# Making the fourth feed-forward sequence's products during the last steps of the latent attention

## The reference

```python
x = x + _L0_xattn_ref(_layernorm(x), ctx_512, ctx_512)
x = x + _L0_ffn_ref(_layernorm(x), ...)                  # routed experts
x = x + _L1_xattn_ref(_layernorm(x), ctx_512, ...)       # latent attention, 16 heads
x = x + _L1_ffn_ref(_layernorm(x), w_gate, w_up, w_down) # this case is about its start
```

```python
gate = _mx_linear(x, w_gate)        # 256 -> 1024
up = _mx_linear(x, w_up)
inter = jax.nn.silu(gate) * up
return _mx_linear(inter, w_down)    # quantises inter, 1024 -> 256
```

## Time and profile before

| | |
|---|---|
| median of 3 runs | 785.99 us |
| lowest and highest | 784.54, 786.02 us |
| the profiled execution, its own time | 785.92 us |
| its span, from the first to the last instruction | 783.9 us |
| busy, share of the span: PE, DVE, POOL, ACT | 94%, 75%, 72%, 52% |
| mean granted clock of TensorE | 0.991 of full speed |

### The profile page before, as it was taken

The page is one execution under the profiler, slowest core; times in us unless marked ns, Lnnn a source line. Parts: engine busy times, 40 slices in busy tenths (PEclk is TensorE's granted clock), DMA queues, the critical chain, the costliest instruction groups (busy, mean ns, idle before and its releaser), DMA issues.

```text
span 783.9 us, 15005 instructions
## 1 busy us (share of the span) xinstructions
PE 733.1 (94%) x4872; PEld 534.6 (68%) x4872; DVE 589.0 (75%) x1077; ACT 405.2 (52%) x1084; POOL 564.7 (72%) x588
## 2 busy tenths in 40 slices
PE   3999999978999999798999999999999999987896
PEld 2655555446888888766787777777777777755554
DVE  5898888948777778776565677676767676768996
ACT  1678878732333233326454454655455544573664
POOL 5667777525777767665757778888788888766895
PEclk9999999979999999999999999999999999999999
DMA  9300000013000001132110000000000000000101
GB/s 252 136 1 0 0 0 1 2 52 127 21 21 21 20 22 59 37 125 102 51 52 1 1 2 1 2 1 1 1 1 2 2 1 2 1 1 2 35 28 48
DMA packets 8764, 24.14 MB, mean 31 GB/s; under 512 B 1711, under 2 KB 5167, under 8 KB 8087
## 3 DMA queue, kind: packets, MB, share of 16 engines
q1 hardware_dynamic: 8154, 23.28, 9.0%
q10 hardware_dynamic: 549, 0.08, 0.1%
HBM read 21.26 MB, written 2.10 MB: 30 GB/s over the span
## 4 chain that ended last, share of the span: by engine, by line
PE 44%; DVE 6%; issue 3%; ACT 3%; POOL 2%; DVEq 0%; POOLq 0%; ACTq 0%
PE ps L1413 17%; PE ps L1462 5%; PE ps L1483 4%; PE ps L1429 4%; PE ps L1447 4%; PE ps L1432 3%; PE ps L1497 3%; PE ps L1324 2%; DVE ps L2172 1%; DVE f_h L2160 1%; ACT p L1573 1%; POOL f_h L2280 1%; ACT f_gated L2124 1%; PE ps L2046 1%; ACT l_y L1563 0%
## 5 line engine op out<-in xcount | busy, mean ns | idle before, releaser
L1758 POOL TENSOR_TENSOR q<-turned 64x512 f32<-64x512 f32 x127 | 166.2, 1309 | 24.2 <-DVE turned L1677 11.4
L1413 PE MATMUL ps<-l_yt,a 128*128 128x512 f32 x576 | 144.1, 400 | 4.0 <-DVE a L1631 2.3
L1413 PEld LDWEIGHTS ps<-l_yt,a 128*128 128x128 f32 x576 | 105.1, 189 | 28.9 <-DVE a L1631 2.9
L1745 POOL TENSOR_TENSOR p<-p,l_inverse 128x512 f32<-128x512 f32 x64 | 66.4, 1040 | 60.1 <-DVE l_inverse L1699 59.2
L1677 DVE TENSOR_TENSOR turned<-ps,rope 128x1024 f32<-128x1024 f32 x64 | 78.0, 1219 | 40.6 <-PE ps L1413 36.3
L881 PE MATMUL ps<-yt_experts,wsplit 128*128 (+1 forms) x384 | 97.3, 403 | 0.1
L468 DVE TENSOR_REDUCE negmax<-ps 128x4 f32<-128x512 f32 x128 | 85.1, 685 | 14.9 <-PE ps L291 13.8
L1573 ACT ACTIVATE p<-ps,l_negmax 128x128 f32<-128x128 f32 x256 | 89.8, 388 | 6.5 <-DVE l_negmax L1668 6.5
L881 PEld LDWEIGHTS ps<-yt_experts,wsplit 128*128 128x128 f32 x384 | 71.6, 193 | 14.5 <-DVE inner L1036 0.3
L384 ACT ACTIVATE pt<-ps 128x512 f32<-128x512 f32 x128 | 69.8, 599 | 5.5 <-PE ps L313 3.7
L1590 ACT ACTIVATE qs<-ps 128x512 f32<-128x512 f32 x32 | 19.1, 597 | 102.6 <-PE ps L1432 102.6
(11 more groups left out here) (231 smaller groups left out, 1563.0 us busy)
## 6 DMA issues: line engine op xcount, KB each, us to landing
wide<-in_wide SPq DMA_DIRECT2D x8, 768.0 KB, 4.3
mx_raw<-in_mx SPq DMA_DIRECT2D x8, 384.0 KB, 3.1
x<-in_x SPq DMA_DIRECT2D x4, 512.0 KB, 8.9
ctx_t<-in_ctx_t SPq DMA_DIRECT2D x1, 2048.0 KB, 7.8
out<-x SPq DMA_DIRECT2D x16, 128.0 KB, 1.7
narrow<-in_narrow SPq DMA_DIRECT2D x8, 192.0 KB, 4.1
ktraw<-in_ctx_rows SPq DMA_DIRECT2D x1, 1248.0 KB
wraw<-in_gate SPq DMA_DIRECT2D x1, 1024.0 KB, 18.7
```

Of the source, the lines that this page charges most:

```text
L1413: out = pe.matmul(tile_bank(n, k), a[i][:, pa, kin, k * 128:(k + 1) * 128], yt[j % 2][:, py, kin, :, :].rearrange("p b s -> p (b s)"), sta ...
L1745: pool.tensor_tensor(p[:, head, :, :], p[:, head, :, :], spread(inverse[:, head, :], 2, S), ALU.mult).then_inc(normed[head], 1)
L1758: t = pool.tensor_tensor(out[rows[(head + half) % 2], head, :], turned[rows[head], half, :], turned[rows[head], 2 + half, :], ALU.add)
```

## The change

`EARLY` goes from 3 to 4. On PE the gate products of sequence 3 come ahead of `turn_p(END)`, its up products ahead of `project(END)`; they go to the banks 0 and 7, so they no longer wait for the last context's split, which `products(4, 1)` does now. The first turning, of `hq(0)`, waits for `combine(3)` instead of `combine(2)`. `combine(3)` reads its two up banks in two halves. On ACT `silu(3)` and `invert_scale(2)` are written ahead of the loop, where they stood as the loop's first instructions: the order of ACT's queue is the same.

```diff
@@ feed_forward
-    EARLY = 3
+    EARLY = 4
     gate_bank = lambda n, half: m.bank(2 + half)
     up_bank = lambda n, half: m.bank((0, 7 if n < EARLY else 1)[half])
@@ tensor
         products(2, 0)
         products(2, 1)
+        products(3, 0)
         turn_p(END, 0)
         turn_p(END, 1)
         project(END - 1, 0)
         project(END - 1, 1)
         context(END)
+        products(3, 1)
         project(END, 0)
         project(END, 1)
         steps(pe, body)
@@ scalar, body
             if n >= EARLY and inside(n, B):
                 silu(n)
-            if n >= 3 and inside(n - 1, B):
+            if n >= EARLY and inside(n - 1, B):
                 invert_scale(n - 1, (place - 1) % 4)
@@ scalar
         keep_context(END)
+        silu(3)
+        invert_scale(2, 2)
         steps(act, body)
```

## The result

The changed kernel takes 782.45 us in the median of 5 runs (781.26 to 783.34) where the kernel before takes 785.99 (784.54 to 787.58): ratio 0.9947, 95% interval 0.9928 to 0.9966, so 0.5% faster, 3.5 us. The forecast was 786.2, no difference that can be told, and its range ended at 783.2. It came out as rival 1, and somewhat better than that rival's 783.3.

A forecast was written before the change was run, and what follows sets the result against it. DVE and POOL were taken to set the pace in the feed-forward's steady run. SiLU(3)'s 3.2 us gain is swallowed by waiting for POOL; net +0.2 to +0.3 on 785.92 gives 786.2, range 783.2 to 786.9.

The forecast's parts named there:

- rival 1: `clip(1)` on DVE gets between POOL's `hq(0)` and sequence 2's quantising; `combine(3)` 1.61 earlier, -2.7 us, 783.3; chance 0.27.
- L2221's fate: At `clip(1)`: DVE waits for both overlapping POOL instructions, as the late rescaling had; it ends at 715.20, `combine(3)` +0.25.
- The other bound: At `clip(1)`: DVE gets between the two POOL instructions, ending at 712.26 + 1.08 = 713.34.
- pause of 3.25 us: PE idles 713.2 to 716.45 before the turning of `hq(0)`; clock falls there, back for `down(0)`; net +0.2 us.
- The head: Steps up to `combine(3)`: `turn_p(END)` at 706.58, +1.12; SiLU(3) at 710.65, 3.2 us earlier.
- the winning branch: The case of rival 1, `clip(1)` getting between the POOL instructions: `combine(3)` at 713.26, -1.61 us.
- The two pauses in PE: If `clip(1)` gets between the POOL instructions, PE pauses 0.8 and 1.4 us, so the clock stays up and `down(0)` is fast.
- The clock: If PE's clock stays up for `down(0)`, DVE and POOL give back later idle time, up to 1.1 us.
- Rival 3: After a 3.25 us pause PE stays at 1.2 GHz twice as long, over sequences 5 and 6: +3.1, 789.1; chance 0.05.

The follow-up runs named there:

- experiment 2: The changed kernel with the lower limit of `clip(1)` taken from PSUM instead of SBUF, run twice: 780.30 us (ratio 0.9920), then 781.69 (0.9936).

## Why the prediction was wrong, point by point

| drain, us | kernel |
|---|---|
| 81.6 | before; `combine(3)` at +14.8 from `combine(0)`; clock falls ahead of `down(0)` |
| 80.1 | before with both pauses filled; `combine(3)` at +14.8; clock stays up |
| 78.6 | after; `combine(3)` at +13.2; clock stays up |
| 77.9 | after, `clip(1)` with one SBUF input; `combine(3)` at +12.5 |

- **The step that failed** is "I choose L2221's fate: `clip(1)` waits for both, 714.12 + 1.08 = 715.20". It got between: 711.99 + 1.08 = 713.07. The other bound had it at 713.34, 0.3 later as all times of that profile are. One lost contest was taken for a property of two POOL instructions that overlap in the record. The rescaling, the instruction that had lost, won the same contest in the changed kernel, with POOL's first half running for 0.56 us instead of 0.24. The Trainium skill's rule of issue order (SBUF — State Buffer, section "Who interferes with whom") gave the right outcome at `clip(1)`; L2221 contradicts it only if the start on record of a POOL instruction is also the moment of its issue, which no run here shows.
- **What followed from it** fell too: no pause of 3.25 us, so no fall of the clock at 716.
- **The head** was right on the winning branch: `combine(3)` 1.61 earlier was forecast for rival 1, and 1.58 measured against `combine(0)` (13.24 against 14.82). SiLU(3) and `turn_p(END)` stood at 710.32 and 706.28, with the 0.3 offset 710.6 and 706.6 for a forecast of 710.65 and 706.58. The quantising of sequence 1 took 1.92, as the forecast chose, and not the 2.13 of before. The two pauses in PE were given as 0.8 and 1.4 and measured 1.44 and 1.45.
- **The clock** was seen, with the right sign, and sized too small: at most 1.1 us, the idle time of DVE before `combine` and before the clip. Measured with the order unchanged: 81.57 to 80.11, 1.46. Of that 0.6 are gained by `combine(6)` and 0.2 more by `combine(15)`, within the 1.1. The last 0.65 come at the end, where the rescaling wins against POOL (1.58 instead of 2.90) and DVE comes 0.56 instead of 0.24 us after POOL's first half. That term was missing: the wait was inside a DVE instruction's duration and not in any idle time. In the changed kernel the three parts are 1.58 (`combine(3)`), 0.75 (from there to `combine(15)`) and 0.66 (from there to the end), 2.99 in all; rival 1 had 1.55 and 1.1 and nothing for the last, so it came near the time partly by luck.
- **Half and half**: of the 3.0 us of drain 1.5 come from the clock and 1.5 from the earlier `combine(3)`, if the pauses are filled first and `combine(3)` is moved then. The other order was seen only in part, in the gate products alone: with the clock down an earlier `combine(3)` gave nothing. In medians: 2.0 (786.25 to 784.25) and 1.8 (784.25 to 782.44). Each of these two steps is clear of the noise. The medians say more than one pair of profiles on the first half, because the clock falls in different places from execution to execution.
- **Rival 3** (twice as long at 1.2 GHz) did not come in the changed kernel, but did in the one with the gate products alone, where the old pause of 2.8 us was left: the granted clock was down between 718 and 726 us instead of between 719 and 724. It cost 1.1 us from `combine(3)` to the end (67.85 instead of 66.75), not the 3.1 that the rival gave it.
- **The two halves of the change do different things.** The gate products bring the SiLU forward, the up products let `combine(3)` follow and shorten the pause ahead of `down(0)`. In medians each gains alone, 1.1 and 2.0 us, against 3.5 and 3.8 for both; the intervals are too wide to say that together they give more than their sum.

## What to carry to other kernels

An instruction that reads two SBUF tensors on VectorE beside a busy GpSimd can hold a wait that shows only in its duration (here 1.94 instead of 1.21 us, and 2.90 instead of 1.22): compare its duration with others of its form, and give it a PSUM operand if one is at hand. Who wins such a contest is no constant of the pair; from one row both outcomes stay open, and the chance should say so. And where TensorE is not the bound, its pauses can still count: here what kept its clock up was worth as much as what shortened the path.

The best version that came out is the changed kernel with the limit of `clip(1)` in PSUM: 780.3 and 781.7 us in two jobs, ratios 0.9920 and 0.9936.

## What the runs showed of the hardware that was not expected

- 21 unused matmuls in TensorE's pauses made the kernel 2.0 us faster (786.25 to 784.25). From 700 us on, the pause of 2.83 or 2.84 us was followed by a granted clock of 0.50 in all five profiles that have it unfilled, the one of 2.25 in three of five, the one of 2.53 not in its one profile, and pauses of 0.5 to 1.5 in none (falls behind the last copy to x left aside). The length of a single pause does not decide it alone: in the profile of before the granted clock is 0.50 from 167 to 177 us, and the pauses just ahead were 1.10 (ending at 164.08) and 1.41 (ending at 166.79).
- The place of the fall varies with the execution: the profiles of the kernel before and its near relatives have it at 711, at 718 or at 720 us. The kernel's times spread with the mean granted clock, which counts falls elsewhere too: of 73 runs of the kernel before, 39 had 0.991 and a median of 787.1 us, 30 had 0.993 and 785.6, 2 had 0.996 and 783.1, and 2 had 0.989 and 786.7.
- Two profiles of the changed kernel agree to some 0.03 us from 700 us on, including which engine goes first; the two of experiment 2 agree to 0.02 us in the drain (77.88 and 77.86).
